# Edge batches set between the halves of the pair features, and expert results added straight into the output

## The chip, the cores and the metric

The kernel runs on one core of one Trainium2 chip. The metric is the device time of one execution in microseconds (us); the verdict is a ratio of such times. A core has engines that run at the same time and meet through semaphores: TensorE (PE; matmuls and transposes), VectorE (DVE), ScalarE (ACT), GpSimd (POOL; here mostly issuing indirect DMAs) and SyncE (SP; issuing plain DMAs). Each engine takes its instructions strictly in the order in which the program lists them.

## The reference

One layer on 3125 nodes with 256 features and 50000 edges: a graph attention (4 heads of 64) and a global second-order attention (8 heads of 32) over the normalized nodes, then a mixture of 8 experts of which each node uses 2.

```python
xn = layernorm(x)
h = xn @ W                                       # graph attention, with self loops
e = leaky_relu(a_src[src] + a_dst[dst], 0.2)
alpha = softmax of e over the edges that share dst
gnn = segment_sum(alpha * h[src], dst) + bias
q, k, v = heads of (xn @ Wqkv.T + bqkv)          # second-order attention
y = 0.5 * sum_ij qn_i qn_j (sum_n kn_i kn_j [1, v]) + scale^2 * qn (sum_n kn [1, v]) + scale^4 * sum [1, v]
mix = (y[1:] / y[0]) @ Wproj.T + bproj
x = x + gnn + mix
g = layernorm(x)                                 # experts
p, i = softmax of the top 2 of g @ Wg.T + bg
x = x + sum over the two experts of p * (relu(g @ W1.T + b1) @ W2.T + b2)
```

## The kernel before

The nodes are cut into NT = 25 tiles of 128 rows, the edges into NBT = 110 batches of four groups of 128 edges. The program is one list of instructions for each engine, written out by hand, with semaphores between them. The order of work on an engine is the order of that list, and a wait holds all that stands behind it on that engine.

*Edge batches.* GpSimd's `gather(b)` fetches the source rows of batch b with four indirect DMAs (line 853) into one of NBUF = 8 buffers; from the ninth batch on it first waits until TensorE has used batch b - 8. ScalarE (`weight_columns`, `scaled_messages`, lines 960 and 970) and VectorE (`edge_batches`, lines 1848 and 1853) weight the rows and build one-hots of the destinations. TensorE's `aggregate(b)` (line 1267) multiplies them into two PSUM banks, one for each slot s of the batch. VectorE's `accumulate(b, s)` (lines 1833 to 1838) adds a bank to the sums of a node tile whose number it loads into a register; only then may TensorE write that bank for the next batch. In `edge_batches`, batch b accumulates batch b - 2 around its one-hot, and TensorE's turn for batch b aggregates b - 1.

*Feature steps.* Steps 0 to 28 make the features of the second-order attention, one node tile t after another, as a pipeline over engines: TensorE's `project(t)` (1284), VectorE's `heads(t)` (1783, 1786), ScalarE's `squares`, VectorE's `squares_a` and `squares_b` (1794, 1804), ScalarE's `norms`, VectorE's `unit(t - 2)` (1790 to 1814), ScalarE's `wrap`, `own_squares` and `windows`, VectorE's `pairs(t - 3, g)` for the two halves g of the heads (1829), TensorE's `sums(t - 4)` (1296 to 1303). A half's feature buffer `phi[g]` is free again when `sums` has read it. From step S_EDGE = 8 on each step also handles two edge batches. On VectorE they stand at the end of the step, on TensorE between `project(t)` and the transposes `q_T(t - 2)`, on ScalarE behind `norms`. The four steps after 28 turn the sums into coefficients and handle two batches each.

*Late edge stage.* 57 turns apply the coefficients to all nodes (lines 1463 to 1482, with ScalarE's squares between), each with one or two of the remaining 60 batches.

*Experts.* The sum so far lies in `res`; SP stores it in five parts to `sum_d` in HBM (783) and its normalized form to `xn_d` (779). VectorE then reuses `res` for the slot one-hots (2184 to 2188) that order the tokens by expert. 56 tiles of 128 slots run in a loop: GpSimd's `load_tokens` (887), transposes, two matmul stages (1560, 1570), `results` on VectorE (2214, 2217), and GpSimd's `add_results` (895), which adds the rows to `sum_d` by an indirect DMA that accumulates, after the one before it has landed. Slots without a token point at rows behind the nodes' rows. At the end SP copies `sum_d` to the output (794).

Of the kernel before, what the change touches and what calls it, by code (L numbers as in the profile page):

```python
# [16 lines left out]
P = 128  # L17
# [107 lines left out]
def gps_layer(nc, x, src, dst, wcat, wgt, att_src, att_dst, gbias, bqkv, wpt, bproj, temp,  # L125
# [20 lines left out]
    with ctx:  # L146
# [18 lines left out]
        sum_d = dram("sum_d", [NP + P, D])  # L165
# [500 lines left out]
        def _(sp):  # L666
# [80 lines left out]
            sp.dma_start(sum_d[NP:NP + P, :], zrow).then_inc(s_zero, 16)  # L747
# [33 lines left out]
            for c in range(LC):  # L781
                sp.wait_ge(s_att2, c + 1)
                sp.dma_start(sum_d[c * LW * P:(c + 1) * LW * P, :].rearrange("(t p) c -> p t c", p=P),
                             res[:, c * LW:(c + 1) * LW, :]).then_inc(s_res, 16)
                if c:
                    store_normalized(c - 1)
# [6 lines left out]
            sp.wait_ge(s_fy, 16 * NJ)  # L793
            sp.dma_start(out.rearrange("n c -> (n c)").rearrange("(p w) -> p w", p=P),
                         sum_d[0:N, :].rearrange("n c -> (n c)").rearrange("(p w) -> p w", p=P)).then_inc(s_res, 16)
# [4 lines left out]
        def _(pool):  # L800
# [78 lines left out]
            pool.wait_ge(s_zero, 32)  # L879
# [10 lines left out]
            def add_results(j):  # L890

                if j:
                    pool.wait_ge(s_fy, 16 * j)
                pool.wait_ge(s_fw, j + 1)
                pool.indirect_dma_start(sum_d, bass.IndirectOffsetOnAxis(pidx[:, j:j + 1], 0),  # L895
                                        ys[j % 2], None, compute_op=ALU.add).then_inc(s_fy, 16)
            for j in range(JB - 1):
                load_tokens(j)
            pool.wait_ge(s_res, 16 * LC)
# [8 lines left out]
        def _(act):  # L908
# [64 lines left out]
            def edge_columns(step):  # L973
                for b in edges(step):
                    weight_columns(b)
                    scaled_messages(b)
# [57 lines left out]
            for step in range(S_T):  # L1034
# [3 lines left out]
                if 0 <= t - 3 < NT:  # L1038
                    own_squares(t - 3)
                if 0 <= t - 1 < NT:  # L1040
                    norms(t - 1)
                if step > S_BULK:
                    edge_columns(step)
                if t < NT:
                    squares(t)
                if T_KP <= t - 2 < NT:
                    windows(t - 2)
# [26 lines left out]
            for step in range(S_T, S_A):  # L1074
                edge_columns(step)
# [20 lines left out]
            for n in range(ZR + 1):  # L1096
                if n < ZR:
                    squares_of_sums(n)
                edge_columns(S_A + n)
# [46 lines left out]
        def _(pe):  # L1146
# [124 lines left out]
            def edge_sums(step):  # L1271
                for b in edges(step):
                    if b:
                        aggregate(b - 1)
# [12 lines left out]
            def sums(t):  # L1287

                n = P if t < NT - 1 else TAIL
                e_ = ext[t % XE]  # L1290
                kw = dict(stop=(t == NT - 1), skip_group_check=True)
                for g in range(KD):
                    pe.wait_ge(s_ksq, KD * t + g + 1)
                    pe.wait_ge(s_phi, KD * t + g + 1)
                    for h in range(QC):
                        MM(ps[h * MD:(h + 1) * MD, g, :], vb[t % VB][0:n, (g * QC + h) * MD:(g * QC + h + 1) * MD],  # L1296
                           phi[g][0:n, h, :], start=(t == 0), **kw)
                    for h in range(QC):
                        MM(ps[h * MD:(h + 1) * MD, 2, g * P:g * P + 2 * MD + 1],
                           vb[t % VB][0:n, (g * QC + h) * MD:(g * QC + h + 1) * MD], e_[0:n, g * QC + h, 0:2 * MD + 1],  # L1300
                           start=(t == 0 and g == 0), **kw)
                    for h in range(QC):
                        last = MM(ps[h * MD:(h + 1) * MD, 2, g * P + 2 * MD + 1:g * P + 3 * MD + 2],  # L1303
                                  e_[0:n, g * QC + h, MD + 1:2 * MD + 1], e_[0:n, g * QC + h, MD:2 * MD + 1], start=False, **kw)
                    last.then_inc(s_kv, 1)
# [64 lines left out]
            for step in range(S_T):  # L1370
                t = step
                if t >= 4:
                    sums(t - 4)
# [4 lines left out]
                if t < NT:  # L1378
                    project(t)
                edge_sums(step)  # L1380
# [3 lines left out]
                if 0 <= t - 2 < NT:  # L1384
                    q_T(t - 2)
                if 0 <= step - S_SCAN < 4:
                    neighbours(step - S_SCAN + 1)
# [6 lines left out]
            edge_sums(S_T)  # L1394
# [8 lines left out]
            edge_sums(S_T + 1)  # L1403
# [6 lines left out]
            edge_sums(S_T + 2)  # L1410
            pe.wait_ge(s_kvc, 3)
            pe.wait_ge(s_wpt, 16)
            edge_sums(S_T + 3)
# [70 lines left out]
            for n in range(ZR + 1):  # L1484
# [7 lines left out]
                edge_sums(S_A + n)  # L1492
# [84 lines left out]
        def _(dve):  # L1577
# [262 lines left out]
            def edge_batches(step):  # L1840
                for b in edges(step):
# [87 lines left out]
            def bulk_weights():  # L1929
# [12 lines left out]
                dve.wait_ge(s_zero, 32)  # L1942
# [10 lines left out]
            for step in range(S_T):  # L1953
# [9 lines left out]
                if 0 <= t - 1 < NT:  # L1963
                    summed = squares_a(t - 1)
                    squares_b(t - 1, summed)
                if 0 <= t - 3 < NT:
                    pairs(t - 3, 1)
# [8 lines left out]
                edge_batches(step)  # L1976
# [16 lines left out]
            edge_batches(S_T)  # L1993
# [4 lines left out]
            edge_batches(S_T + 1)  # L1998
# [5 lines left out]
            edge_batches(S_T + 2)  # L2004
            edge_batches(S_T + 3)
# [30 lines left out]
            for n in range(ZR + 1):  # L2036
                r, c = n // NQC, n % NQC
                edge_batches(S_A + n)
# [141 lines left out]
            dve.wait_ge(s_res, 16 * LC)  # L2180
# [77 lines left out]
```

## Time and profile before

| | us |
|---|---|
| median of 3 runs | 1449.74 |
| lowest and highest | 1444.14, 1452.1 |
| the profiled execution, its time | 1443.35 |
| its span | 1441.3 |
| TensorE, VectorE, GpSimd, ScalarE busy in it | 1202.2, 847.1, 669.3, 609.0 |

The profile is one execution of the program. Its rows give start and length in us, an engine, a line of the kernel (L853), an operation and what it writes and reads. An idle time in brackets ends with the work that released the instruction. The chain of waits follows the work that ended last back to the start. TensorE's granted clock is a share of its full 2.4 GHz; 0.5 is its lower level.

### The profile page before, as it was taken

The page shows a single profiled execution, that of the slowest core. Times are in us where ns is not written, and L with a number is a line of the kernel's source. Part 1 is how long each engine was busy: PE and PEld are TensorE (multiplying, and loading weights), DVE is VectorE, ACT ScalarE, POOL GpSimd, SP SyncE. Part 2 cuts the span into 40 slices and gives each one's busy share as a digit, 9 for nine tenths or more (in the row PEclk, how much of TensorE's full clock was granted, in tenths as well). Part 3 has the DMA queues.
Part 4 walks back from the last instruction along what each step waited for, and adds up shares of the span by engine and source line. Part 5 has one row for each costly group of instructions (what it writes and reads, how often), then busy time and mean ns, then how long its engine had stood idle before and what let it go on. Part 6 is the DMA issues. An engine that isn't in the chain of part 4 may idle for free.

```text
span 1441.3 us, 25299 instructions
## 1 busy us (share of the span) xinstructions
PE 1202.2 (83%) x7992; PEld 865.4 (60%) x7993; DVE 847.1 (59%) x1771; ACT 609.0 (42%) x1967; POOL 669.3 (46%) x626
## 2 busy tenths in 40 slices
PE   3789956748778877899999999275999999999994
PEld 2645533425444544545455556174899999999994
DVE  8599859788888887644545446878222233332221
ACT  1400011444554446587777777250333333333331
POOL 2070000675556556777777777630333333333331
PEclk9999966779988988999999999657999999999997
DMA  5635374432222223333434333773122222222223
GB/s 178 213 121 198 140 283 140 141 94 74 79 83 82 78 80 92 99 114 100 117 114 117 103 115 113 289 277 131 31 36 37 37 36 36 36 36 36 36 36 103
DMA packets 67570, 153.67 MB, mean 107 GB/s; under 512 B 12962, under 2 KB 41559, under 8 KB 66263
## 3 DMA queue, kind: packets, MB, share of 16 engines
q0 software_dynamic: 32640, 75.27, 21.0%
q1 hardware_dynamic: 33478, 74.93, 14.7%
q10 hardware_dynamic: 1360, 2.33, 0.5%
q8 instruction: 47, 0.77, 0.2%
q14 instruction: 45, 0.36, 0.1%
HBM read 131.76 MB, written 23.92 MB: 108 GB/s over the span
## 4 chain that ended last, share of the span: by engine, by line
PE 66%; DVE 20%; issue 4%; DMA 3%; POOL 2%; ACT 1%; DVEq 1%; SPq 0%; POOLq 0%; ACTq 0%
PE ps L1267 15%; PE ps L1560 14%; PE ps L1570 13%; DVE arena L1829 4%; PE ps L1463 4%; PE ps L1208 4%; PE ps L1475 3%; PE ps L1296 2%; PE ps L1217 1%; PE ps L1421 1%; DVEq L1833 1%; PE ps L1175 1%; POOL arena L853 1%; DVE arena L1786 1%; DMA h_d<-arena 1%
## 5 line engine op out<-in xcount | busy, mean ns | idle before, releaser
L853 POOL DMA_INDIRECT arena<-h_d,tables x440 | 449.1, 1021 | 189.5 <-issue 126.1
L1267 PE MATMUL ps<-arena 128*128 128x264 f32 x880 | 246.1, 434 | 86.2 <-DVE acc L1838 63.6
L1267 PEld LDWEIGHTS ps<-arena 128*128 128x128 f32 x880 | 181.2, 214 | 143.9 <-issue 91.4
L970 ACT ACTIVATE arena<-arena 128x64 f32<-128x64 f32 x880 | 222.0, 339 | 17.6 <-DMA arena<-h_d,tables 17.6
L1560 PE MATMUL ps<-acc 128*128 128x128 f32 x1792 | 211.3, 277 | 0.0
L895 POOL DMA_INDIRECT sum_d<-acc,tables x56 | 89.8, 1603 | 254.9 <-DVE acc L2217 247.4
L1560 PEld LDWEIGHTS ps<-acc 128*128 128x128 f32 x1792 | 206.5, 193 | 0.3
L1570 PE MATMUL ps<-arena,acc 128*128 x896 | 202.5, 379 | 0.0
L1137 ACT ACTIVATE acc<-ps,b_s 128x128 f32<-128x128 f32 x448 | 128.1, 369 | 120.1 <-PE ps L1560 120.1
L1570 PEld LDWEIGHTS ps<-arena,acc 128*128 128x128 f32 x896 | 166.0, 190 | 20.3
L2205 DVE COPY acc<-arena 128x1024 f32 x112 | 78.3, 700 | 123.8 <-PE ps L1560 123.3
L1838 DVE TENSOR_TENSOR acc<-acc,ps 128x264 f32 x220 | 93.5, 425 | 72.6 <-PE ps L1267 61.6
L1084 ACT ACTIVATE arena<-ps 128x1024 f32<-128x1024 f32 (+1 forms) x112 | 98.3, 930 | 77.3 <-PE ps L1463 77.3
L2214 DVE TENSOR_TENSOR acc<-ps,arena 128x256 f32<-128x256 f32 x56 | 23.8, 425 | 162.7 <-PE ps L1570 162.7
L1829 DVE TENSOR_TENSOR arena<-arena,ps 128x1920 f32<-128x1920 f32 x40 | 85.8, 2150 | 24.8 <-PE ps L1303 24.8
L1128 ACT COPY acc<-ps 128x256 f32<-128x256 f32 x56 | 20.9, 373 | 171.5 <-PE ps L1549 171.5
L887 POOL DMA_INDIRECT acc<-xn_d,tables x56 | 56.3, 1006 | 76.2 <-DVE tables L2195 59.5
L1208 PE MATMUL ps<-arena 128*100 128x392 bf16 x384 | 74.5, 344 | 9.7 <-DVE arena L1770 8.0
L1284 PE MATMUL ps<-arena 128*128 128x512 f32 (+1 forms) x200 | 80.1, 548 | 0.0
L1853 DVE TENSOR_TENSOR arena<-arena 128x512 f32<-128x512 f32 x110 | 75.6, 687 | 4.8 <-DMA arena<-h_d,tables 4.6
L1770 DVE SCALAR_TENSOR_TENSOR arena<-arena,ps 100x392 f32<-100x392 uint8 x128 | 71.5, 615 | 8.7 <-PE ps L1208 8.6
L1848 DVE TENSOR_TENSOR arena<-iota_f,tables 128x512 f32<-128x512 f32 x110 | 75.3, 685 | 0.0
(368 smaller groups left out, 1489.6 us busy)
## 6 DMA issues: line engine op xcount, KB each, us to landing
arena<-dl_d SPq DMA_DIRECT2D x22, 640.0 KB, 6.9
arena<-lo_d SPq DMA_DIRECT2D x16, 784.0 KB, 4.4
arena<-h_d,tables POOLq DMA_INDIRECT x440
arena<-in_w SPq DMA_DIRECT2D x4, 1664.0 KB, 11.7
arena<-in_w SPq DMA_DIRECT2D x4, 1632.0 KB, 25.5
arena<-hi_d SPq DMA_DIRECT2D x16, 343.0 KB, 5.1
h_d<-arena SPq DMA_DIRECT2D x25, 128.0 KB, 1.7
sum_d<-res SPq DMA_DIRECT2D x5, 640.0 KB, 7.9
```

What stands on the lines that cost most here:

```text
L853: pool.indirect_dma_start(gb[u][:, k, 0:D], None, h_d, bass.IndirectOffsetOnAxis(tsrc[:, j:j + 1], 0)).then_inc(s_gg[u], 16)
L895: pool.indirect_dma_start(sum_d, bass.IndirectOffsetOnAxis(pidx[:, j:j + 1], 0), ys[j % 2], None, compute_op=ALU.add).then_inc(s_fy, 16)
L970: ins = A_.activation(v, v, ACT.Copy, scale=wm[:, m + k, h:h + 1])
L1084: A_.activation(zsq[n % 2][:, 2 * half:2 * half + 2, 0:w], ps[:, 2 * half:2 * half + 2, 0:w], ACT.Square)\
L1137: last = A_.activation(hT[u][:, c, :], ps[:, 1 + 2 * u + n_, (c % 4) * P:(c % 4 + 1) * P], ACT.Relu, bias=b1_s[:, ds(ej * HC + c, 1)])
L1208: last = MM(ps[0:NT * GH, n % 5, 0:EP], tsp[:, s, :], lob[i // 2 % LB][:, col], start=(s == 0), stop=(s == 2))
L1267: last = MM(ps[:, 6 + s, 0:ACOL], oh[b % OB][:, m, :], gb[u][:, m, :], start=(k == 0), stop=(k == TE - 1))
L1284: last = MM(o_, xT[:, k, t * P:(t + 1) * P], wq_s[:, k, s], start=(k == 0), stop=(k == KD - 1))
L1560: last = MM(ps[:, 1 + 2 * (u % 2) + n_, c * P:(c + 1) * P], w1c[n_][:, k, c * P:(c + 1) * P], xfT[u % 2][:, k, :], start=(k == 0), stop=(k ...
L1570: last = MM(ps[:, 5 + u % 2, 0:D], hT[u % 2][:, c, :], w2_s[:, ds(e, 1), c, :].rearrange("p o n -> p (o n)"), start=(c == 0), stop=(c == H ...
L1829: V.tensor_tensor(phi[g].rearrange("p h (r i) -> p h r i", i=MD)[:, :, 1:SQ], k0, k1, ALU.mult).then_inc(s_phi, 1)
L1838: V.tensor_tensor(q, q, ps[:, 6 + s, 0:ACOL], ALU.add).then_inc(s_accd, 1)
```

## The change

In feature steps from step 8 on, VectorE handles the step's first edge batch before the second half of the pairs, and its second batch at the end. TensorE takes the sums of one half, a batch, the sums of the other half, the transposes, the second batch and the projection of the next tile; the sums belong to the pairs of the same step instead of those of the step before. ScalarE puts its norms between the two batches and the windows ahead of the squares. Outside these steps the batches are listed as before. The table of summed rows `sum_d` goes: SP stores `res` to the output in six parts, and the experts add into the output, with indices past the last row left out by a bounds check. The copy at the end goes, and with it one clearing store at the start.

```diff
-        sum_d = dram("sum_d", [NP + P, D])
@@ SP
-            sp.dma_start(sum_d[NP:NP + P, :], zrow).then_inc(s_zero, 16)
...
             for c in range(LC):
                 sp.wait_ge(s_att2, c + 1)
-                sp.dma_start(sum_d[c * LW * P:(c + 1) * LW * P, :].rearrange("(t p) c -> p t c", p=P),
-                             res[:, c * LW:(c + 1) * LW, :]).then_inc(s_res, 16)
+                a, b = c * LW, min((c + 1) * LW, NT - 1)
+                sp.dma_start(ot[:, a:b, :], res[:, a:b, :]).then_inc(s_res, 16)
+                if c == LC - 1:
+                    sp.dma_start(out[(NT - 1) * P:N, :], res[0:TAIL, NT - 1, :]).then_inc(s_res, 16)
                 if c:
                     store_normalized(c - 1)
...
-            sp.wait_ge(s_fy, 16 * NJ)
-            sp.dma_start(out.rearrange("n c -> (n c)").rearrange("(p w) -> p w", p=P),
-                         sum_d[0:N, :].rearrange("n c -> (n c)").rearrange("(p w) -> p w", p=P)).then_inc(s_res, 16)
             sp.wait_ge(s_res, 16 * (LC + 1))
@@ GpSimd
-                pool.indirect_dma_start(sum_d, bass.IndirectOffsetOnAxis(pidx[:, j:j + 1], 0),
-                                        ys[j % 2], None, compute_op=ALU.add).then_inc(s_fy, 16)
+                pool.indirect_dma_start(out, bass.IndirectOffsetOnAxis(pidx[:, j:j + 1], 0),
+                                        ys[j % 2], None, bounds_check=N - 1, oob_is_err=False,
+                                        compute_op=ALU.add).then_inc(s_fy, 16)
...
-            pool.wait_ge(s_res, 16 * LC)
+            pool.wait_ge(s_res, 16 * (LC + 1))
@@ ScalarE
                     own_squares(t - 3)
+                edge_columns(edges(step)[0:1])
                 if 0 <= t - 1 < NT:
                     norms(t - 1)
-                if step > S_BULK:
-                    edge_columns(step)
+                edge_columns(edges(step)[1:])
+                if T_KP <= t - 2 < NT:
+                    windows(t - 2)
                 if t < NT:
                     squares(t)
-                if T_KP <= t - 2 < NT:
-                    windows(t - 2)
@@ TensorE
-            def sums(t):
+            def sums(t, groups=range(KD)):
...
-                if t >= 4:
+                if 4 <= t <= S_EDGE:
                     sums(t - 4)
...
-                if t < NT:
+                if t <= S_EDGE:
                     project(t)
-                edge_sums(step)
+                if S_EDGE <= t < NT + 3:
+                    sums(t - 3, (0,))
+                edge_sums(edges(step)[0:1])
+                if S_EDGE <= t < NT + 3:
+                    sums(t - 3, (1,))
...
                 if 0 <= t - 2 < NT:
                     q_T(t - 2)
+                edge_sums(edges(step)[1:])
+                if S_EDGE <= t < NT - 1:
+                    project(t + 1)
@@ VectorE
                     squares_b(t - 1, summed)
+                edge_batches(edges(step)[0:1])
                 if 0 <= t - 3 < NT:
                     pairs(t - 3, 1)
                 if t < NT:
                     heads(t)
...
-                edge_batches(step)
+                edge_batches(edges(step)[1:])
...
-            dve.wait_ge(s_res, 16 * LC)
+            dve.wait_ge(s_res, 16 * (LC + 1))
```

`edge_columns`, `edge_sums` and `edge_batches` now take the list of batches instead of the step; the waits on `s_zero` go from 32 to 16.

## Rows read from the trace of the kernel before

**Rows 1.** Stretches by stage: busy us of each engine, granted clock, DMA share, GB/s
```profile
312.00:580.00 268.00, 208.14 (x1482) 132.57 (x1482) 219.75 (x380) 134.68 (x538) 161.93 (x167) 0.87 0.29 82
620.00:910.00 290.00, 283.05 (x1613) 156.26 (x1612) 147.24 (x312) 213.92 (x627) 218.47 (x217) 1.00 0.38 111
...
1060.00:1420.00 360.00, 359.10 (x2466) 335.07 (x2465) 106.04 (x196) 129.95 (x440) 125.40 (x96) 1.00 0.22 35
```

**Rows 2.** Chain that ended last: start us, us, what
```profile
330.32 2.15 DVE arena L1829
336.76 5.49 PE ps L1267 x16
343.71 2.15 DVE arena L1829
...
528.45 2.15 DVE arena L1829
...
903.31 3.76 DMA arena<-h_d,tables
```

**Rows 3.** Timeline of GpSimd: start us, us, instruction, idle before it
```profile
327.16 0.94 POOL L853 DMA_INDIRECT arena<-h_d,tables  x1 [4.71 <-PE ps L1267]
...
562.11 0.94 POOL L853 DMA_INDIRECT arena<-h_d,tables  x1 [1.92 <-PE ps L1267]
```

**Rows 4.** GpSimd's gather line alone, 562 to 905 us: length, busy us
```profile
562.00:905.00 343.00, 263.25 (x260) 0.99 0.38 109
```

**Rows 5.** Timeline of VectorE, feature steps 7 to 9
```profile
304.27 0.25 DVE L1790 RECIPROCAL arena<-arena 128x16 f32<-128x16 f32 x1 [1.32 <-issue]
...
305.65 2.15 DVE L1829 TENSOR_TENSOR arena<-arena,ps 128x1920 f32<-128x1920 f32 x1
...
318.43 2.15 DVE L1829 TENSOR_TENSOR arena<-arena,ps 128x1920 f32<-128x1920 f32 x1 [3.05 <-PE ps L1303]
...
321.21 0.18 DVE L1804 TENSOR_TENSOR arena<-arena 128x16 f32<-128x16 f32 x1
321.30 2.15 DVE L1829 TENSOR_TENSOR arena<-arena,ps 128x1920 f32<-128x1920 f32 x1
...
324.30 0.42 DVE L1838 TENSOR_TENSOR acc<-acc,ps 128x264 f32 x1
...
328.06 0.25 DVE L1790 RECIPROCAL arena<-arena 128x16 f32<-128x16 f32 x1
```

**Rows 6.** Line 1833, the load of a tile number: ns min/median/max
```profile
L1833 DVEq TENSOR_LOAD <-ts_row x220: 296/303/565, 322.2 to 910.5; - x110
```

**Rows 7.** Timeline of VectorE in the later edge stage
```profile
702.17 0.42 DVE L2034 TENSOR_TENSOR res<-res,ps 128x256 f32<-128x256 f32 x1 [1.82 <-PE ps L1421]
703.01 0.43 DVE L1838 TENSOR_TENSOR acc<-acc,ps 128x264 f32 x1 [0.41 <-issue]
```

**Rows 8.** Timeline of TensorE, feature step 9
```profile
324.86 3.90 PE L1267 MATMUL ps<-arena 128*128 128x264 f32 x16 [2.71 <-DVE acc L1838]
...
331.12 2.85 PE L1284 MATMUL ps<-arena 128*128 128x512 f32 x8
```

**Rows 9.** Timeline of all engines, end of the span
```profile
1424.52 1.55 POOL L895 DMA_INDIRECT sum_d<-acc,tables  x1 [2.46 <-DMA sum_d<-acc,tables]
1428.35 0.60 SPq L794 DMA_DIRECT2D out<-sum_d  x1
```

**Rows 10.** DMA issues of the page: count, KB each, median us to landing
```profile
out<-sum_d SPq DMA_DIRECT2D x1, 3125.0 KB, 12.5
```

**Rows 11.** Line 895, the scatter: ns min/median/max, first and last start
```profile
L895 POOL DMA_INDIRECT sum_d<-acc,tables x56: 1549/1586/1989, 1027.2 to 1424.5; - x56
```

**Rows 12.** Line 783, the stores of the sums: issues, landing
```profile
L783 SPq DMA_DIRECT2D sum_d<-res x5: 359/377/947, 929.9 to 960.9; - x5
...
DMA to landing us min/median/max: 3.9/7.9/18.8
```

**Rows 13.** Chain that ended last, 898 to 1016 us
```profile
985.67 1.36 DVE acc L2184
```

More of the change, by code:

```diff
@@ L876, in _ @@
                 ins.then_inc(s_own, 1)
-            pool.wait_ge(s_zero, 32)
+            pool.wait_ge(s_zero, 16)
             pool.wait_ge(s_xst, 16 * LC)
@@ L971, in scaled_messages, with edge_columns @@
                 ins.then_inc(s_wc, 1)
-            def edge_columns(step):
-                for b in edges(step):
+            def edge_columns(batches):
+                for b in batches:
                     weight_columns(b)
@@ L1074, in _ @@
             for step in range(S_T, S_A):
-                edge_columns(step)
+                edge_columns(edges(step))
             def squares_of_sums(n):
@@ L1098, in _ @@
                     squares_of_sums(n)
-                edge_columns(S_A + n)
+                edge_columns(edges(S_A + n))
             act.wait_ge(s_fin, 1)
@@ L1269, in aggregate, with edge_sums @@
                     last.then_inc(s_agg, 1)
-            def edge_sums(step):
-                for b in edges(step):
+            def edge_sums(batches):
+                for b in batches:
                     if b:
@@ L1291, in sums @@
                 kw = dict(stop=(t == NT - 1), skip_group_check=True)
-                for g in range(KD):
+                for g in groups:
                     pe.wait_ge(s_ksq, KD * t + g + 1)
@@ L1391, in _ @@
                         slot_words(p)
-            edge_sums(S_T)
+            edge_sums(edges(S_T))
             pe.wait_ge(s_kvc, 1)
@@ L1402, in _ @@
             last.then_inc(s_cft, 1)
-            edge_sums(S_T + 1)
+            edge_sums(edges(S_T + 1))
             pe.wait_ge(s_kvc, 2)
@@ L1409, in _ @@
             last.then_inc(s_cft, 1)
-            edge_sums(S_T + 2)
+            edge_sums(edges(S_T + 2))
             pe.wait_ge(s_kvc, 3)
             pe.wait_ge(s_wpt, 16)
-            edge_sums(S_T + 3)
+            edge_sums(edges(S_T + 3))
             def mix_out(m):
@@ L1838, in accumulate, with edge_batches @@
                 V.tensor_tensor(q, q, ps[:, 6 + s, 0:ACOL], ALU.add).then_inc(s_accd, 1)
-            def edge_batches(step):
-                for b in edges(step):
+            def edge_batches(batches):
+                for b in batches:
                     u = b % NBUF
@@ L1941, in bulk_weights @@
                 dve.wait_ge(s_we, 1)
-                dve.wait_ge(s_zero, 32)
+                dve.wait_ge(s_zero, 16)
                 dve.wait_ge(s_bias, NT)
@@ L1992, in _ @@
             ins.then_inc(s_kvc, 1)
-            edge_batches(S_T)
+            edge_batches(edges(S_T))
             dve.wait_ge(s_cft, 1)
@@ L2003, in _ @@
             ins.then_inc(s_kvc, 1)
-            edge_batches(S_T + 2)
-            edge_batches(S_T + 3)
+            edge_batches(edges(S_T + 2))
+            edge_batches(edges(S_T + 3))
             def gram_terms(r):
@@ L2037, in _ @@
                 r, c = n // NQC, n % NQC
-                edge_batches(S_A + n)
+                edge_batches(edges(S_A + n))
                 if c == 0 and r < RQ:
```

4 lines of the change are left out of this document (2 added, 2 removed).

## The prediction

> **What bounds the kernel now.** I read the stretches by stage first, then the chain of waits through one feature step, then each engine's order of time. The stages differ [rows 1]. From 312 to 580 us (the feature steps) no engine is full: TensorE 208 of 268 us at a mean granted clock of 0.87, VectorE 220, GpSimd 162. From 620 to 910 TensorE is busy 283 of 290 us, from 1060 to 1420 (experts) 359 of 360. After that comes only the end of the output.
>
> A feature step is a ring of VectorE and TensorE [rows 2]. VectorE multiplies pair half 0 (L1829), half 1, adds the heads' biases, and only then reaches its first edge accumulate (L1838). That accumulate frees the PSUM bank on which TensorE's two edge batches wait (5.49 us from 336.76); transposes and the sums of older pairs stand behind them on TensorE, and these sums free the feature buffer that the next half 0 overwrites. One turn, from 330.32 to 343.71, is 13.4 us. Half 0 of steps 9 and 25 starts at 318.43 and 528.45 [rows 2, 5], so the 16 turns between average 13.13.
>
> GpSimd shows what that costs. In every feature step its gathers wait once for TensorE to release a buffer, first until 327.16, last until 562.11 [rows 3]. From there 260 gathers (65 batches) follow one another [rows 4] up to 903.31, where the landing of the last one is in the chain [rows 2]: 341.2 us for 64.75 batches, 5.27 each. So the gathers set the end of the edge work, and a feature step that is faster counts up to GpSimd's last wait. TensorE is nearly as full in that stretch, but its start there moves forward with the features too.
>
> **The change, part by part.** *Feature steps.* VectorE now does half 0, edge batch A, half 1, heads, edge batch B. TensorE does the sums of half 0 of this same step's pairs (one step younger than before), the batch before A, the sums of half 1, transposes, A itself, then the projection for the next step. ScalarE puts its norms between the batches. No arithmetic is added. I walk one step, with the start of half 0 as zero.
>
> VectorE without waits: from 318.43 to the reciprocal at 328.06 it has 9.63 us with no wait inside, and from the reciprocal at 304.27 to half 0 at 305.65 1.38 [rows 5]; together 11.0. The new order adds one thing. Each accumulate begins with a load of its tile number into a register (303 ns) and some register work [rows 6]. Before, these loads ran ahead under half 1's 2.15 us. Now the first stands right behind a short maximum (L1804), which waits for its own reduce, so nothing covers the load. The nearest rows are in the later stage: an add that has waited starts at 702.17, the accumulate behind it at 703.01, with 0.41 of idle before it [rows 7]: 0.84 from start to start. Half 1 starts 0.09 after L1804 today [rows 5], so the hole costs about 0.74. Bounds: 0 (the loads run ahead after all) and 1.5 (both batches pay). I take 0.74, since A has lost its cover and B still has half 1 as before: 11.76 us per step.
>
> The Trainium skill (page "DMA: Bandwidth & Descriptors", section "Latency and other measured facts") puts the floor of a `tensor_load` at about 600 ns, which speaks against one on the path. By it the hole would be an estimated 0.3 us larger, and the end 5 us later. The trace's 303 ns decides, and the sum goes without the page.
>
> Does TensorE keep up? In the step from 324.86, where the two batches took 3.90, batches, transposes and sums take 6.26 and the projection 2.85 [rows 8]: 9.1 of 11.76. Half 0 ends at 2.15; its sums take some 1.2 (half of 6.26 - 3.90), to 3.3. The first accumulate starts at 2.78 (L1804) + 0.84 = 3.6, and a batch starts 0.56 after its accumulate (324.30, 324.86) [rows 5, 8]: the batch before A runs from 4.2 to 6.1. VectorE's batch takes 1.88 (half of 324.30 to 328.06), so half 1 runs from 5.5 to 7.7, and its sums with the transposes to 9.1; A runs to 11.05, the projection to 13.9, which is 2.1 of the next step, just before its sums can begin. Half 1 and heads take 3.0 (321.30 to 324.30), so VectorE's B asks at 8.5 for the batch done at 6.1; the heads ask at 7.6 for a projection done at 2.1; the next A asks at 3.6 for a batch done 4.3 earlier. On TensorE gaps of 0.9 and 1.6 remain. With the clock at its lower level for a stretch, the two batches take 5.49 instead of 3.90 [rows 2, 8]; that 1.6 fits into the gaps. ScalarE is busy 135 of 268 [rows 1], about 7 us a step, which fits between its requests. GpSimd needs 10.5 us a step and still waits about 1.
>
> Sum to the gathers' end. Step 8 has no accumulate yet and so no hole, and half 0 of step 9 loses its wait of 3.05 [rows 5]: 315.4 instead of 318.43. Sixteen turns of 11.76 put step 25 at 503.5 instead of 528.45: 25 us earlier. Step 25 has no heads (3.0 less half 1's 2.1), so step 26 starts 10.8 later. The release for which GpSimd waits last (step 25's second batch) comes 6.1 into it, at 16.9 after step 25's start; two batches later, at 27.5, stands the gather that now stands at 562.11, which is 33.7 after. That adds 6.2. Together 31 us; the 65 batches behind it cost what they cost now. Bounds: without the hole 16 x 0.74 more, 43 (had GpSimd no wait at all from the first one on, the 102 batches from 322.6, 4.6 before 327.16, would end 44 earlier: the ceiling); with both holes 19.
>
> *Output.* The results are stored to the output and the experts add there, so the last copy goes. It is issued at 1428.35, once the scatter of 1424.52 has landed [rows 9], and takes 12.5 us to land [rows 10]; 0.45 closes the span at 1441.3. The end becomes 1428.8, a gain of 12.5. Added is a bounds check in each scatter, as padding slots lie beyond the output's rows. The trace has no checked indirect DMA; nearest are the unchecked scatters, 1549 to 1989 ns, median 1586 [rows 11]. I bound the check at -0.2 (skipped rows are not moved) and +1.6 (it doubles the scatter), and take 0, at the unchecked median. Only the last two scatters are on the path: the last has waited 2.46 for the landing before it, a cycle of 4.0 [rows 9]; the others have 7.22 us per tile (1027.2 to 1424.5, 56 scatters) [rows 11] against that 4.0. So -0.4 to +3.2 us.
>
> The output's last rows need one more store on SP's queue, behind the last of five at 960.9 [rows 12]. Behind it there stand the last two stores of normalized rows, the last weight loads and the expert biases; the next of them waits for ScalarE anyway, which hides its issue of 0.4 us (the cost without that cover). GpSimd and VectorE now wait for six stores; VectorE before the slot one-hots at 985.67 [rows 13], with the permutation matmuls and the token loads behind them. With the longest landing, 18.8 us [rows 12], the last store is down at 980: nothing. One clearing store less and the shorter wait for it are no gain, since no chain goes through them.
>
> Sum: 31 + 12.5 = 43.5 us. The profiled execution took 1443.35 (span 1441.3), so 1399.9 there; it lies 6.4 below the median of the three runs, 1449.74, from which I get 1406.2.
>
> **The rivals.**
> (1) TensorE's clock takes the place of the wait. Now it falls about once per step, after the one gap of some 2.7 us. If it falls in both new gaps, a step is 9.1 + 2 x 1.6 = 12.3 us: gain 3 + 16 x 0.83 + 6.2 = 22.5, with the copy 35, end 1415. For it: the 0.87 of these steps. Against: the batches of 324.86 took 3.90 although TensorE had waited 2.71 before them [rows 8], and the new gaps are shorter. The Trainium skill ("TensorE: Matmul & The Clock Gate", "A second HAM failure mode: psum-queue depth-cycling") warns that short idles between groups of matmuls make the clock swing; by it this case is the one to expect. Chance 0.18.
> (2) No hole: the loads run ahead. Gain 43 + 12.5, end 1394. Chance 0.12.
> (3) The ring only changes its place: TensorE's sums now wait for this step's halves, and if VectorE then waits for B as long as it did for half 0, the step stays at 13.1 and only the copy is won: 1437. Against it stand the slacks of 2.4 and more above. That the changed order isn't what the engines then follow is part of it. Chance 0.08.
> (4) Slower: checked scatters are slow on GpSimd. A tile lasts 7.22 us, a scatter's cycle 4.0; from 3.2 us of extra cost it binds, 56 tiles pay each further us, and at 4.0 the 43.5 is gone. At 5 us extra: 56 x 1.8 = 100, less 43.5, end 1506. No scatter in the trace takes over 2 us. Chance 0.04.
>
> **How the numbers follow.** The forecast, 1406, has 0.58; its own range is 1400 to 1412 (a hole of 0.5 to 1.0, the scatter's bounds). The range takes in (1) and (2), both holes (1418) and some us between runs: 1390 to 1420; (3) and (4) are left out. A measurement of this kernel can tell about 0.5%, 7 us, from no change. Slower is (4), 0.04; no change is (3) with a step a little longer than 13.1, 0.03; faster is the rest, 0.93.
>
> **What would show it.** Right: steps of 11.8 us between first halves, a gap of some 0.7 before A's accumulate and none before half 0, GpSimd's waits near 1 us, its last gather near 873, the span ending some 4 us after the last scatter's start. Steps of 11.0 show (2); batches of 5.49 twice a step with VectorE waiting for TensorE show (1); scatters over 5 us (4). If the gathers' end moves but little although the steps are short, TensorE was the bound of the late stretch, and my reading of GpSimd is wrong.

## The result and the profile after

| | before | after |
|---|---|---|
| median, us (runs) | 1448.01 (4) | 1405.74 (4) |
| lowest and highest | 1444.14, 1452.1 | 1404.29, 1407.52 |
| profiled execution: time, span | 1443.35, 1441.3 | 1404.77, 1403.0 |
| step 8's half 0, start | 305.65 | 304.11 |
| last gather, start | 903.31 | 869.51 |
| last scatter, start | 1424.52 | 1393.65 |

The ratio is 0.9704, 95% interval [0.9685, 0.9723]: 42.3 us faster by the medians, where 1406 was forecast for 1405.74.

By stretches (columns as in [rows 1]): the feature steps at a granted clock of 0.97 instead of 0.87, the later edge stage and the experts with TensorE as nearly full as before. TensorE's busy share of the feature steps did not grow; the stretch became shorter.

```profile
303.00:536.00 233.00, 179.66 (x1454) 111.56 (x1454) 219.69 (x379) 137.69 (x539) 165.14 (x165) 0.97 0.33 95
557.00:870.00 313.00, 307.36 (x1745) 168.06 (x1743) 159.97 (x338) 233.82 (x680) 239.86 (x241) 1.00 0.38 111
...
1027.00:1393.00 366.00, 363.29 (x2481) 337.76 (x2479) 109.38 (x199) 131.10 (x444) 129.44 (x98) 1.00 0.21 33
```

One feature step on VectorE, from its timeline. L1834 is the half multiply (L1829 before), L1843 the accumulate (L1838), L1809 the short maximum (L1804).

```profile
384.48 2.14 DVE L1834 TENSOR_TENSOR arena<-arena,ps 128x1920 f32<-128x1920 f32 x1
386.55 0.67 DVE L1799 TENSOR_REDUCE arena<-arena 128x16 f32<-128x512 f32 x1
387.25 0.18 DVE L1809 TENSOR_TENSOR arena<-arena 128x16 f32<-128x16 f32 x1
388.08 0.43 DVE L1843 TENSOR_TENSOR acc<-acc,ps 128x264 f32 x1 [0.65 <-issue]
...
389.97 2.15 DVE L1834 TENSOR_TENSOR arena<-arena,ps 128x1920 f32<-128x1920 f32 x1
...
392.97 0.42 DVE L1843 TENSOR_TENSOR acc<-acc,ps 128x264 f32 x1
...
396.25 2.14 DVE L1834 TENSOR_TENSOR arena<-arena,ps 128x1920 f32<-128x1920 f32 x1
```

From half 0 at 384.48 to the next at 396.25 it is 11.77 us, and no row but one, in the whole timeline between them, has idle time before it. That one is the hole: 0.65 us before the first accumulate, put down to "issue", which means that the engine waited for no other. In it lie the load of the tile number and the register work behind it, from the list of line 1838 (387.0 to 388.2 us; ns, then first and last start; the second load is that of the next accumulate):

```profile
L1838 DVEq TENSOR_LOAD <-ts_row x2: 308/308/309, 387.3 to 388.1; - x2
L1838 DVEq FUSED_REGOPS  x1: 190/190/190, 387.6 to 387.6; - x1
```

Nothing stands before half 0, where [rows 5] had 3.05. Sixteen such steps lead from step 9's half 0 (313.75) to step 25's (502.08): 11.77 each, where [rows 2, 5] gave 13.13.

The same step on TensorE (L1294 and L1301 are sums, L1265 a batch, L1282 the projection):

```profile
386.77 1.06 PE L1294 MATMUL ps<-arena 128*32 128x512 f32 x8 [0.29 <-DVE arena L1834]
...
388.66 2.02 PE L1265 MATMUL ps<-arena 128*128 128x264 f32 x8 [0.65 <-DVE acc L1843]
392.27 1.07 PE L1294 MATMUL ps<-arena 128*32 128x512 f32 x8 [1.59 <-DVE arena L1834]
...
393.71 1.95 PE L1265 MATMUL ps<-arena 128*128 128x264 f32 x8
395.50 2.74 PE L1282 MATMUL ps<-arena 128*128 128x512 f32 x8
```

TensorE waits three times for VectorE, and VectorE never for TensorE: the ring is gone, and VectorE's own work sets the step. Both batches run at the full level of 2.4 GHz (2.02 and 1.95 us; the pair took 3.90 to 5.49 in [rows 2, 8]): from step 9's half 0 to step 25's the granted clock is 1.00, where it was 0.89 before.

GpSimd (answering to [rows 3]) waits about 1.64 us once a step, for the last time for longer than 0.3 us until 509.49 instead of 562.11, and its last gather starts 33.8 us earlier than before:

```profile
390.95 0.95 POOL L850 DMA_INDIRECT arena<-h_d,tables  x1 [1.64 <-PE ps L1265]
...
509.49 0.95 POOL L850 DMA_INDIRECT arena<-h_d,tables  x1 [2.58 <-PE ps L1265]
...
869.51 0.95 POOL L850 DMA_INDIRECT arena<-h_d,tables  x1 [0.30 <-issue]
```

The checked scatters as a group (ns min/median/max, first and last start, then landing in us) stand beside the unchecked of [rows 11], 1549/1586/1989: the scatter itself is not longer with the check. The last line is the landing of the unchecked ones.

```profile
L892 POOL DMA_INDIRECT out<-acc,tables x56: 1551/1587/1879, 996.1 to 1393.7; - x56
...
DMA to landing us min/median/max: 2.7/3.8/4.3
```

```profile
DMA to landing us min/median/max: 3.6/3.9/5.8
```

The end is where the profile after differs from what was written. The last scatter, from GpSimd's timeline, and the instruction with which GpSimd closes its program, from the list of line 146 (the block's end; ns, then its start):

```profile
1393.65 1.55 POOL L892 DMA_INDIRECT out<-acc,tables  x1 [2.48 <-DMA out<-acc,tables]
```

```profile
L146 POOLq DRAIN  x1: 6269/6269/6269, 1396.5 to 1396.5; - x1
```

The same row of the kernel before, which none of the groups ahead of the prediction holds:

```profile
L146 POOLq DRAIN  x1: 6267/6267/6267, 1428.5 to 1428.5; - x1
```

GpSimd leaves its list once the last scatter has landed (1396.4) and then drains for 6.27 us; the drain ends at 1402.75 and the span at 1403.0. Before, the same drain ran from 1428.5 to 1434.8, under the 12.5 us of the copy [rows 9, 10], where it cost nothing. Thus the end stands 9.35 us after the last scatter's start (1403.0 - 1393.65) and not 4.3; before it stood 16.78 after (1441.3 - 1424.52). So the end gives 7.4 us. Of these 6.3 are the copy less the drain: from the landing to the end of the span it is 6.6 (1403.0 - 1396.4), where it was 12.95 (1441.3 - 1428.35). The other 1.1 is the last landing, 2.75 us after the scatter's start instead of 3.83 (the shortest landings of the 56 are 2.7 and 3.6 in the lines above). The kernel with the new output alone has 2.7 there too, that with the new order alone 3.6; whether the rows that the check leaves out are the reason was not tried.

Where the profiled pair's 38.3 us of span (1441.3 - 1403.0) went: 1.5 lie ahead of step 8 (305.65 - 304.11); 32.3 from there to the last gather (597.66 against 565.40); -2.9 from the last gather to the last scatter (521.21 against 524.14); 7.4 at the end.

### The profile page after: what moved, and what is told of

Same layout as the page of the kernel before. It is cut to its first block, busy times and chain, and to the rows that moved or that the text cites. A ratio compares the mean times of both kernels' runs of the same rounds, so it can differ in the third digit from the quotient of the medians.

```text
span 1403.0 us, 25354 instructions
## 1 busy us (share of the span) xinstructions
PE 1183.3 (84%) x7992; PEld 850.7 (61%) x7993; DVE 846.9 (60%) x1771; ACT 610.8 (44%) x1967; POOL 672.7 (48%) x626
## 4 chain that ended last, share of the span: by engine, by line
PE 58%; DVE 25%; issue 6%; DMA 4%; POOL 2%; DVEq 2%; ACT 2%; SPq 0%; POOLq 0%; ACTq 0%
PE ps L1565 13%; PE ps L1575 13%; PE ps L1265 8%; DVE arena L1834 5%; PE ps L1206 4%; PE ps L1468 4%; PE ps L1480 3%; DVE acc L1843 2%; PE ps L1215 2%; DVEq L1838 2%; POOL arena L850 1%; PE ps L1426 1%; PE ps L1173 1%; DVE arena L1858 1%; DMA h_d<-arena 1%
## 5 line engine op out<-in xcount | busy, mean ns | idle before, releaser
L1265 PE MATMUL ps<-arena 128*128 128x264 f32 x880 | 220.5, 395 | 23.6 <-DVE acc L1843 17.3
L892 POOL DMA_INDIRECT out<-acc,tables x56 | 89.4, 1597 | 255.3 <-DVE acc L2223 247.7
L1265 PEld LDWEIGHTS ps<-arena 128*128 128x128 f32 x880 | 160.6, 192 | 65.6 <-issue 40.7
L1843 DVE TENSOR_TENSOR acc<-acc,ps 128x264 f32 x220 | 93.2, 424 | 54.6 <-PE ps L1265 30.9
L1294 PE MATMUL ps<-arena 128*32 128x512 f32 (+1 forms) x400 | 60.8, 680 | 48.7 <-DVE arena L1834 48.7
L1858 DVE TENSOR_TENSOR arena<-arena 128x512 f32<-128x512 f32 x110 | 75.4, 685 | 32.3 <-DMA arena<-h_d,tables 32.1
L1834 DVE TENSOR_TENSOR arena<-arena,ps 128x1920 f32<-128x1920 f32 x40 | 85.8, 2145 | 0.0
L1282 PE MATMUL ps<-arena 128*128 128x512 f32 (+1 forms) x200 | 75.9, 525 | 0.0
```

Source lines behind the costliest of these rows:

```text
L892: pool.indirect_dma_start(out, bass.IndirectOffsetOnAxis(pidx[:, j:j + 1], 0), ys[j % 2], None, bounds_check=N - 1, oob_is_err=False, comp ...
L1265: last = MM(ps[:, 6 + s, 0:ACOL], oh[b % OB][:, m, :], gb[u][:, m, :], start=(k == 0), stop=(k == TE - 1))
L1834: V.tensor_tensor(phi[g].rearrange("p h (r i) -> p h r i", i=MD)[:, :, 1:SQ], k0, k1, ALU.mult).then_inc(s_phi, 1)
L1843: V.tensor_tensor(q, q, ps[:, 6 + s, 0:ACOL], ALU.add).then_inc(s_accd, 1)
L1858: V.tensor_tensor(v, v, over(wm[:, m:m + KA, 0:GH], GD), ALU.mult).then_inc(s_msg, 1)
```

## The experiments

All were timed beside the kernel before on the same chip. Executions differ in how long they take to reach step 8 (its half 0 starts between 302.44 and 309.80 in the kernels of the table, though little was edited ahead of it: one clearing store), so the table also gives the profiled execution from that half 0 to the end of the span.

| kernel | median, us | ratio and interval | step 8 to the end |
|---|---|---|---|
| before | 1448.0, 1447.1, 1446.8 | | 1135.7 |
| after | 1405.74 | 0.9704 [0.9685, 0.9723] | 1098.9 |
| order only | 1413.83 | 0.9762 [0.9736, 0.9788] | 1104.7 |
| output only | 1438.88 | 0.9940 [0.9922, 0.9959] | 1136.8 |
| after, maximum behind the batch | 1391.01 | 0.9603 [0.9574, 0.9631] | 1087.9 |
| after, VectorE not split | 1400.57 | 0.9684 [0.9650, 0.9719] | 1093.1 |
| after, GpSimd leaves early | 1408.45 | 0.9734 [0.9711, 0.9758] | 1100.0 |
| after, three gathers of four | 1401.93 | 0.9681 [0.9654, 0.9708] | 1093.6 |
| after, maximum and early leaving | 1389.35 | 0.9600 [0.9579, 0.9622] | 1084.8 |

The theory: VectorE's own work sets the feature step; its one hole is a load that nothing covers; the faster steps count up to the gathers; and the end is held by GpSimd's drain. The rivals: the hole is the price of something else in the accumulate; TensorE and not the gathers sets the later stage; the drain is the landing of a DMA under another name.

### The two halves of the change alone

**Order only**: the kernel before with the new order on VectorE, TensorE and ScalarE; `sum_d`, its stores and the copy stay. VectorE's part of the edit:

```diff
+                edge_batches(edges(step)[0:1])
                 if 0 <= t - 3 < NT:
                     pairs(t - 3, 1)
...
-                edge_batches(step)
+                edge_batches(edges(step)[1:])
```

> The kernel before with the new order of the feature steps alone; the sums still go to their own table and are copied at the end. My theory: the order is worth what the gathers' end moved, 33.8 us less the 1.5 by which that execution was already ahead, so about 1448 - 32 = 1416 us, with steps of 11.76 us. The closing drain of GpSimd (6.27 us) lies under the last copy here. Rival: part of the gain comes only with the new output (fewer stores ahead of the experts); then this run gains under 28 us.

Measured: 1413.83 us, 33.3 under the kernel before; 31.0 by the stretch from step 8 (1135.7 - 1104.7). Its steps are 11.75 (half 0 at 388.48 and 400.23), its last gather starts at 874.23. At the end the copy is issued at 1400.71 and GpSimd's drain lies under it (SP's timeline, then the list of line 146):

```profile
1400.71 0.60 SPq L794 DMA_DIRECT2D out<-sum_d  x1
```

```profile
L146 POOLq DRAIN  x1: 6267/6267/6267, 1400.9 to 1400.9; - x1
```

**Output only**: the kernel before with the experts adding into the output; the order of the steps stays. Of the edit, the copy that goes:

```diff
-            sp.dma_start(out.rearrange("n c -> (n c)").rearrange("(p w) -> p w", p=P),
-                         sum_d[0:N, :].rearrange("n c -> (n c)").rearrange("(p w) -> p w", p=P)).then_inc(s_res, 16)
```

> The kernel before with the new output alone. My theory: without the copy the span ends with GpSimd's drain of 6.27 us, which starts once the last scatter has landed; the end then lies 9.4 us behind the last scatter's start instead of 16.8, a gain of 7.4 us, 1440.6. Rival, the prediction as it stands: the end lies 4.3 us behind it, a gain of 12.5, 1435.5. A third: checked scatters cost the experts' loop time, then under 5 us.

Measured: 1438.88 us, 8.2 under the kernel before. The end, in GpSimd's timeline and the list of line 146:

```profile
1429.78 1.55 POOL L892 DMA_INDIRECT out<-acc,tables  x1 [2.72 <-DMA out<-acc,tables]
```

```profile
L146 POOLq DRAIN  x1: 6269/6269/6269, 1432.7 to 1432.7; - x1
```

With the copy gone the drain is exposed here too: the span ends at 1439.2, 9.4 after the scatter's start, without any change to the order. By the medians the two parts add up: 33.3 + 8.2 = 41.5, beside 42.3 for both. So the term of the order was sized well (31.0 to 33.3 for 31), that of the copy was not: 12.5 lies outside the interval of this run, 5.9 to 11.3.

The profiled execution of this kernel shows no gain from step 8 on (1136.8 for 1135.7), and its timeline of VectorE shows where 3.2 us of it went: in the old order a step lasts 13.4 us when TensorE's batches run at the lower clock and 11.9 when not, and 1 of its 16 steps is of the short kind, against 3 of 16 in the execution of before, so that the 16 take 213.25 us for 210.02. Its last gather is 603.2 us after step 8's half 0 for 597.7. What the output brings is read behind the gathers: from the last one to the end of the span it is 538.0 us before and 538.4 with the order only, 533.6 with the output only and 533.5 in the changed kernel: 4.4 to 4.9 us, of the 7.4 that the end gives. The median's 8.2 lies above that; between 4.4 and 8.2 the runs leave it open.

### The hole

**Maximum behind the batch**: the changed kernel with `squares_b`, whose short maximum waits for its own reduce, behind the step's first edge batch instead of ahead of it. The load of the tile number then stands behind the long half 0.

```diff
-                    squares_b(t - 1, summed)
                 edge_batches(edges(step)[0:1])
+                if 0 <= t - 1 < NT:
+                    squares_b(t - 1, summed)
```

> The changed kernel with the short maximum (L1809) moved behind edge batch A, so that no wait stands ahead of the load of A's tile number. If the hole of 0.65 us of idle is that load behind that wait, steps go from 11.76 to 11.02 us and the gathers end some 11 us earlier (GpSimd without any wait caps it): 1394 to 1396 us. If the hole belongs to the accumulate itself, steps stay at 11.76 and the time at 1405.7. If TensorE, which has only 0.29 us to spare ahead of half 0's sums, becomes the bound, steps lie between.

Measured: 1391.01 us, 14.7 under the changed kernel by the medians, 11.0, as expected, by the stretch from step 8 (the profiled execution is the slowest of its four, 1397.86). VectorE's timeline, then the list of line 1838 from 394 to 397 us:

```profile
394.01 2.14 DVE L1834 TENSOR_TENSOR arena<-arena,ps 128x1920 f32<-128x1920 f32 x1
396.08 0.68 DVE L1799 TENSOR_REDUCE arena<-arena 128x16 f32<-128x512 f32 x1
396.67 0.42 DVE L1843 TENSOR_TENSOR acc<-acc,ps 128x264 f32 x1
...
398.55 0.17 DVE L1809 TENSOR_TENSOR arena<-arena 128x16 f32<-128x16 f32 x1
398.64 2.15 DVE L1834 TENSOR_TENSOR arena<-arena,ps 128x1920 f32<-128x1920 f32 x1
...
404.91 2.14 DVE L1834 TENSOR_TENSOR arena<-arena,ps 128x1920 f32<-128x1920 f32 x1
```

```profile
L1838 DVEq TENSOR_LOAD <-ts_row x1: 298/298/298, 394.1 to 394.1; - x1
```

The accumulate starts 0.59 after the start of the reduce before it, with no idle, and the step is 10.90 us. The load now starts at 394.1, under half 0. The same instructions, two places swapped, and 0.87 us a step are gone: the hole was the load and its register work behind a waiting instruction, nothing in the accumulate itself. Of the 0.87 the hole is 0.74 (0.83 less the 0.09 by which half 1 still starts behind L1809); 0.11 more is the maximum's own wait, 0.70 behind the reduce's start, where 0.59 is enough for the accumulate. The reduce itself is in front of the batch still; only what waits for it has moved.

### Does VectorE's split matter?

**VectorE not split**: the changed kernel, but VectorE does both batches at the end of the step again. TensorE and ScalarE keep the new order.

```diff
-                edge_batches(edges(step)[0:1])
                 if 0 <= t - 3 < NT:
                     pairs(t - 3, 1)
...
-                edge_batches(edges(step)[1:])
+                edge_batches(edges(step))
```

> The changed kernel with both of VectorE's edge batches at the end of the step again; TensorE and ScalarE keep the new order with its younger sums. If the younger sums alone break the ring, VectorE never waits and has no hole: steps of 11.0 us, 1394 to 1396 us. If it is the split on VectorE that breaks it, the first accumulate at 5.9 us of the step holds TensorE back for 3.1 us, its clock falls, the batch takes 3.9 us instead of 1.95, and VectorE's second batch waits for it: steps of about 12.8 us, some 1422 us.

Measured: 1400.57 us, a little under the changed kernel (the intervals overlap). Neither expectation held whole: half 0 starts at 395.12, 406.14 and 418.08, steps of 11.02 and 11.94; 6 of 16 are of the longer kind, and the mean is 11.37. In such a step (VectorE's timeline, then TensorE's, with the first batch of the step before):

```profile
414.00 0.43 DVE L1843 TENSOR_TENSOR acc<-acc,ps 128x264 f32 x1
...
415.76 0.43 DVE L1843 TENSOR_TENSOR acc<-acc,ps 128x264 f32 x1 [0.73 <-PE ps L1265]
```

```profile
401.55 2.02 PE L1265 MATMUL ps<-arena 128*128 128x264 f32 x8 [1.93 <-DVE acc L1843]
...
412.56 3.06 PE L1265 MATMUL ps<-arena 128*128 128x264 f32 x8 [1.92 <-DVE acc L1843]
415.55 1.66 PE L1294 MATMUL ps<-arena 128*32 128x512 f32 x8
```

TensorE has waited 1.92 us for VectorE, its batch then takes 3.06 instead of 2.0, and VectorE's accumulate waits 0.73 for it; the stretch from 303 to 540 has a mean granted clock of 0.91. The wait alone does not decide it: the batch at 401.55 took 2.02 after one of 1.93. Of the 16 steps nine have such a wait of 1.92 or 1.93, and five of these nine a batch of 2.60 to 3.16; the sixth slow batch, 3.56, followed a wait of 2.90. What follows: the ring is broken without VectorE's split, by an order in which TensorE takes the sums of this step's pairs around the first batch; no half 0 of these steps waits for TensorE. (ScalarE keeps its new order here too; its share was not taken apart.) VectorE's split gains nothing over that. It costs the hole, and what it seems to buy is that TensorE's waits are shorter and its batches stay at the full clock. With the hole moved away it is the better of the two, 1391.01 for 1400.57.

### The gathers

**Three gathers of four**: the changed kernel, where GpSimd fetches three of the four groups of a batch from batch 50 on, so that a quarter of the source rows of these batches is left out. The waits of ScalarE and VectorE count the gathers accordingly (not shown).

```diff
-                for k in range(SB * TE):
+                for k in range(SB * TE if b < early else SB * TE - 1):
```

> The changed kernel, but from batch 50 on GpSimd fetches only three of the four groups of rows of a batch: a quarter of the source rows of the late batches is left out, all arithmetic stays. Theory of the prediction (the gathers set the end of the late edge stage): with a quarter of their work gone they no longer do; VectorE's waits for gathers (18.2 us in 13 between 557 and 870) vanish and the stage ends earlier, by at most what TensorE has free there, 313 - 307.4 = 5.6 us, and by the 2 to 3 us in which the last batch stands alone behind the last landing: 4 to 8 us, a time of 1398 to 1402. Rival (TensorE sets the end of the stage, and gathers only seem to): within 1 us of 1405.7. If the gathers alone had set the end with nothing close behind, a quarter of 313 us, over 70 us, would go: 1330.

Measured: 1401.93 us, 3.8 under the changed kernel's median (the intervals overlap); 5.3 by the stretch from step 8, of which 3.6 lie ahead of the first token load (671.9 us after step 8's half 0 before the edit, 668.3 with it) and 1.7 in the experts, which the edit leaves as they are. (VectorE's waits for gathers, from 557 to 870, are 30.3 us in 18; the expectation's 18.2 was too low.) The gather line as a group in the stretch from 557 to 870 (busy us, mean ns, idle before and what ended it), of the changed kernel, with VectorE's message line:

```profile
L850 POOL DMA_INDIRECT arena<-h_d,tables x241 | 241.1, 1001 | 73.4 <-issue 71.0 <-PE ps L1265 2.4
...
L1858 DVE TENSOR_TENSOR arena<-arena 128x512 f32<-128x512 f32 x61 | 41.9, 687 | 30.5 <-DMA arena<-h_d,tables 30.3
```

and of this one, with VectorE's accumulate and message lines:

```profile
L853 POOL DMA_INDIRECT arena<-h_d,tables x185 | 181.0, 978 | 117.9 <-PE ps L1268 73.5 <-issue 44.5
```

```profile
L1846 DVE TENSOR_TENSOR acc<-acc,ps 128x264 f32 x125 | 53.0, 424 | 49.3 <-PE ps L1268 39.2 <-issue 10.0
...
L1861 DVE TENSOR_TENSOR arena<-arena 128x512 f32<-128x512 f32 x62 | 42.5, 685 | 2.6 <-DMA arena<-h_d,tables 2.5
```

GpSimd now waits 73.5 us for TensorE where it waited 2.4, and VectorE 2.5 for gathers where it waited 30.3. TensorE is busy 307.23 of the 313 us, as before (307.36). The last gather starts 546.5 us after step 8's half 0 instead of 565.4, 18.9 earlier, and the stage ends some 4 us earlier. So the gathers did set the end of that stage, as the theory has it, but TensorE stands some 4 us behind them: a quarter of the gathers is worth no more. The size is that of one pair of executions, and by the times alone it is not clear of the noise; that the waits changed engines is.

### The drain

**GpSimd leaves early**: the changed kernel; the last wait for the scatters' landing is SP's.

```diff
@@ SP, at the end
+            sp.wait_ge(s_fy, 16 * NJ)
@@ GpSimd, at the end
-            pool.wait_ge(s_fy, 16 * NJ)
```

> The changed kernel, with GpSimd's last wait (for the landing of the last scatter) given to SP, so that GpSimd leaves its list right after it has issued that scatter; nothing else is changed. In the changed kernel the scatter starts at 1393.65, has landed by 1396.4, GpSimd's closing drain runs 6.27 us from 1396.5 and the span ends at 1403.0, 9.35 after the scatter's start. Theory (the drain is a fixed price of GpSimd's leaving, exposed since no copy covers it any more): it starts about 1.55 after the scatter's start instead of 2.85, and the span ends about 8.0 after it: 1.3 us earlier, 1404.4 by the medians. Rival (the drain waits for the landing of GpSimd's DMAs, or the span's end hangs on something else): the end stays 9.3 to 9.4 after the scatter's start, 1405.7.

Measured: the end moves as the theory says, the time does not show it. The same two views:

```profile
1401.72 1.55 POOL L893 DMA_INDIRECT out<-acc,tables  x1 [2.84 <-DMA out<-acc,tables]
```

```profile
L146 POOLq DRAIN  x1: 8048/8048/8048, 1401.5 to 1401.5; - x1
```

The drain is entered at 1401.5, while the scatter is still to run, and ends at 1409.55: 6.28 after the scatter's end (1401.72 + 1.55). SP, which now waits for the landing, closes its own program at 1404.7, and no scatter lands sooner than 2.7 after its start, here 1404.4; so the drain ends some 5 us after the landing and not 6.27 or more: it goes by GpSimd's own work and not by the landing. The kernel with both edits, below, has the same 8.05 us. The span ends 8.08 after the scatter's start instead of 9.35. The gain of 1.3 is smaller than what executions differ by: this one reached step 8 5.7 us later (309.80), and its median, 1408.45, is above that of the changed kernel. From the last gather to the end it is 532.6 us (1409.8 - 877.20) against 533.5, so 0.9 of the 1.3 remained; the last scatter had waited 2.84 for the one before it, against 2.48.

**Both**: the maximum behind the batch, and GpSimd leaving early.

> The changed kernel with the short maximum moved behind the step's first edge batch (which took the hole out of VectorE's step: 1391.01 us beside 1405.7) and with GpSimd's last wait given to SP. If the two gains lie at different places they add up: 1391.0 less 1.3, 1389.7. If GpSimd's drain waits for landings: 1391.0.

Measured: 1389.35 us, 3.1 under the maximum alone by the stretch from step 8, and again 8.07 from the last scatter's start to the end (1381.33 to 1389.4). That is the fastest of all, 16.4 under the changed kernel; its lead of 1.7 over the maximum alone is within the intervals, so the times cannot tell the sum of both gains from the maximum's alone.

## Why the prediction was right, point by point

**The walk through the step** held to about 0.1 us. With half 0's start (384.48) as zero: the first accumulate at 3.60 (forecast 3.6), the predecessor batch at 4.18 (4.2), half 1 at 5.49 (5.5), its sums at 7.79 (7.7), A from 9.23 to 11.18 (9.1 to 11.05), B's accumulate at 8.49 (8.5), the projection's end at 2.0 of the next step (2.1). The step is 11.77 for 11.76. TensorE's waits are 0.29, 0.65 and 1.59 for 0.9 and 1.6.

**The hole** is 0.65 of idle where 0.41 stood in the row used [rows 7]; from L1809's start to the accumulate it is 0.83 for the 0.84 taken. The choice between 0 and two holes was right: only A pays (B's accumulate at 392.97 has no idle before it). The Trainium skill (page "DMA: Bandwidth & Descriptors", section "Latency and other measured facts") has about 600 ns as the floor of a `tensor_load`; by it the hole was to be an estimated 0.3 larger. The trace after has 296 to 560 ns for these loads, median 303, and steps that agree with 303.

**The gathers' end**: 31 us were forecast and 32.3 measured from step 8 on; the order alone gave 31.4 (597.66 - 566.28). The reading that GpSimd sets the late stage was right, with TensorE some 4 us behind it. That margin was not in the text, and without it the forecast could not have told how much more was to be had.

**The step that was mis-sized is the output's**: "0.45 closes the span at 1441.3", so the end "becomes 1428.8, a gain of 12.5". It took the 0.45 behind the copy for all that stood between the last landing and the end. What lay under the copy was not asked for. GpSimd's drain of 6.27 us was in the trace of before, on line 146, and starts when the last scatter has landed; with the cover of 12.5 gone, 6.3 of the gain was left; a last landing that came 1.1 sooner, which no term had, made it 7.4 at the end of the profiled pair, and the whole output part 8.2 by the medians: the term was 4.3 to 5.1 too large. This is the rule that the prediction applied to the store on SP's queue (what does it cost if the cover is gone) and not to the last copy itself.

**A second, smaller miss**: -2.9 us between the last gather and the last scatter, forecast at 0. (a) 1.5 until the token loads start (106.5 after the last gather, for 105.0). The last batch meets TensorE at the lower clock and takes 2.68 (L1265 at 875.45; the one at 909.21 before took 2.02). Order only has 106.7 and output only 106.5, but the kernel whose VectorE is not split has 105.1 with the new output in it: the 1.5 comes and goes between executions, and no run shows it as a price of either part. (b) 1.2 in the first token tile: 20.1 us from the first load to the first scatter, for 18.9. Its first 32 matmuls take 6.12 for 5.52, and its scatter starts 1.24 after the start of VectorE's last result, for 0.63 (0.63 with the order only as well). In later tiles that distance is 1.24 for 1.13 (1112.19 to 1113.43; 1100.96 to 1102.10 before): with the check a register move of 29 ns stands on GpSimd ahead of each scatter, which the group of line 892 lists 56 times and that of line 895 before does not. That is the price of the check that the traces show, 0.1 us a scatter ahead of it, and off the path, as the tiles stay at 7.23 (7.22 before). Why the first one has 0.6 was not tried. (c) 0.2 in the other 55 tiles.

**Why the number still came out**: the sum was 43.5 and the profiled pair gave 38.3 of span. The medians gave 42.3, since the profiled execution of before was 4.7 us under the median of its four runs and that of after only 1.0 under its own. The forecast carried over 6.4, the distance to the median of the first three, as if it held for both kernels. That is 5.4 too much, and it made up for a sum 4.9 too large (the profiled pair's times differ by 38.6). So the nearness of some 0.3 us is luck; the mechanism and the size of the order's term are what the runs bear out.

**The rivals.** (1) The clock: before, it fell in 13 of the 16 steps from 9 to 25 (those of about 13.4 us, with pairs of batches of 5.44 us and more); in the changed kernel these steps have 1.00 and no pair of batches of 5.49. The Trainium skill ("TensorE: Matmul & The Clock Gate", "A second HAM failure mode: psum-queue depth-cycling") would have the clock swing with short idles between groups of matmuls. The waits of 0.29 to 1.59 here do not show it; the kernel whose VectorE is not split does, with a batch of 2.60 to 3.16 us behind five of its nine waits of 1.92 or 1.93. (2) No hole: the hole was there, and taking it out gave 11 to 14.7 us, 1391 us. The 1394 that the rival named was near that, though it counted the same 12.5 for the copy. (3) The ring in another place: no wait of VectorE for TensorE is left in these steps. (4) Slow checked scatters: 1587 ns for 1586, and 0.1 ahead of each.

## What to carry to other kernels

Before a last transfer is removed, list what else ends after the work that it waits for, closing instructions included: what was hidden under it becomes the end. When work is put between two steps of an engine, look at what stands right ahead of it: here a register load behind a short instruction that waits was exposed, behind a long one it cost nothing, and swapping two neighbours was worth 11 to 14.7 us beside the 42.3 of the whole change. Where two engines both have next to no time to spare in a stage (here TensorE busy 307 of 313 us and GpSimd waiting 2.4), measure how far the second is behind the first before the first is made faster.

## What the runs showed of the hardware

- GpSimd's closing drain took 6.27 us in the seven kernels in which it started with all of GpSimd's work done. Entered while the last scatter was still to run (two kernels), it took 8.05 and ended 6.3 after that scatter's end, some 5 after its landing.
- An indirect DMA with a bounds check took GpSimd 1587 ns in the median and one without it 1586; some 0.1 us was added ahead of it (0.6 ahead of the first).
- The register load (303 ns in the median) and the few register instructions behind it cost VectorE 0.65 us of idle when they stood behind a waiting instruction, and nothing when they could run under a multiply of 2.15 us.
- TensorE's batch of eight matmuls took 2.02 us after waits of 0.65; after waits of 1.92 or 1.93 it took 2.02 four times and 2.60 to 3.16 five times. In the kernel before, the two batches took 3.90 three times and about 5.5 thirteen times after waits of 2.70 to 2.82.
